# A projection moved from step 5 to step 3, and small products added in steps 4 and 12, in a one-core Perceiver layer

## What is computed

```python
Q, K, V = linear(query, Wq, bq), linear(ctx, Wk, bk), linear(ctx, Wv, bv)   # per head: 64 x 16, 1601 x 16
scores = Q @ K.T / sqrt(16)
feats = stack([scores.mean(), scores.max(-1).mean(), var(softmax(scores), ddof=1).mean()])  # per head
t = exp(clip(mlp(feats)))          # three small layers, two exact gelus: a temperature per head
attn = softmax(Q @ K.T / (2 * t))
out = linear(attn @ V, Wo, bo)
```

## Time and profile before

| | |
|---|---|
| median of three runs (lowest to highest) | 1311.03 us (1310.67 to 1316.09) |
| the profiled execution: its time | 1311.66 us |
| its span, first to last instruction | 1309.4 us |
| TensorE busy | 1155.3 us, 88% |
| VectorE, ScalarE, GpSimd busy | 822.0, 768.2, 403.0 us |
| mean granted TensorE clock | 0.861 |

### The profile page before, as it was taken

How to read it: one execution, slowest core, us unless ns; L and a number is a source line. 1 busy time by engine, 2 the same in 40 slices (tenths; PEclk the granted TensorE clock), 3 DMA queues, 4 the chain that set the end, 5 groups by cost and what they waited for, 6 DMA issues and landing times.

```text
span 1309.4 us, 39200 instructions
## 1 busy us (share of the span) xinstructions
PE 1155.3 (88%) x14964; PEld 928.9 (71%) x14964; DVE 822.0 (63%) x2124; ACT 768.2 (59%) x1547; POOL 403.0 (31%) x416
## 2 busy tenths in 40 slices
PE   3767898989899989999899989998999989998935
PEld 3545687868787877878687878787777878776622
DVE  3458665656666766767666766676776766772232
ACT  2434486757666765667566766676566756672300
POOL 2366441313234313333233323431333323301210
PEclk9868697969888987989798988899898979995865
DMA  4500110101010101010110101010101000000000
GB/s 122 187 19 25 29 26 14 54 22 35 14 38 10 50 11 42 19 34 26 26 35 14 46 7 45 11 50 10 42 19 35 26 17 3 3 11 2 2 5 4
DMA packets 46812, 38.85 MB, mean 30 GB/s; under 512 B 14576, under 2 KB 46000, under 8 KB 46640
## 3 DMA queue, kind: packets, MB, share of 16 engines
q1 hardware_dynamic: 46640, 36.41, 10.2%
HBM read 34.30 MB, written 2.10 MB: 28 GB/s over the span
## 4 chain that ended last, share of the span: by engine, by line
PE 65%; DVE 16%; issue 9%; ACT 5%; POOL 2%; DMA 1%; SPq 1%; DVEq 0%; ACTq 0%; POOLq 0%
PE pjp L605 11%; PE pjp L612 11%; PE s2p L677 10%; PE s1p L651 10%; PE pvp L694 7%; DVE est L1185 4%; DVE negm L1179 3%; PE tlp L808 2%; PE tlp L790 2%; PE tlp L784 2%; PE s2p L667 1%; PE tlp L751 1%; PE tlp L771 1%; DVE feat L1202 1%; ACT ering L909 1%
## 5 line engine op out<-in xcount | busy, mean ns | idle before, releaser
L1179 DVE TENSOR_REDUCE negm<-s1p 128x1 f32<-128x400 f32 (+1 forms) x512 | 289.3, 565 | 227.1 <-PE s1p L651 222.5
L909 ACT ACTIVATE ering<-s1p,negm 128x400 f32<-128x400 f32 (+1 forms) x512 | 305.6, 597 | 142.7 <-DVE negm L1179 138.0
L918 ACT ACTIVATE pring<-s2p 128x512 f32<-128x512 f32 (+1 forms) x448 | 251.9, 567 | 152.4 <-PE s2p L677 151.9
L651 PE MATMUL s1p<-kt,qbd 32*128 32x400 f32 (+1 forms) x1024 | 301.0, 597 | 15.8 <-ACT ering L909 13.7
L1185 DVE BATCH_NORM_STATS2 est<-ering 128x6 f32<-128x400 f32 (+1 forms) x512 | 290.3, 567 | 23.4 <-ACT ering L909 23.4
L605 PE MATMUL pjp<-cr,wkv 128*128 128x256 f32 (+1 forms) x1344 | 219.4, 321 | 70.6 <-ACT vt L869 45.7
L605 PEld LDWEIGHTS pjp<-cr,wkv 128*128 128x128 f32 x1344 | 196.1, 223 | 87.8 <-issue 58.5
L677 PE MATMUL s2p<-q2bd,kt 32*128 32x128 f32 (+1 forms) x3328 | 249.7, 284 | 0.0
L677 PEld LDWEIGHTS s2p<-q2bd,kt 32*128 32x128 f32 (+1 forms) x3328 | 240.6, 195 | 7.5
L1083 POOL TENSOR_TENSOR cr<-stage,cr 128x512 fp32r<-128x512 f32 (+1 forms) x112 | 132.0, 1179 | 268.7 <-ACT cr L900 268.7
L612 PE MATMUL pjp<-wkv,cr 128*128 128x256 f32 (+1 forms) x1200 | 191.8, 314 | 11.7 <-ACT kt L882 11.4
(11 more groups left out here) (186 smaller groups left out, 1008.8 us busy)
## 6 DMA issues: line engine op xcount, KB each, us to landing
stage<-in_ctx SPq DMA_DIRECT2D x96, 256.0 KB, 2.9
qbd<-q_dram SPq DMA_DIRECT2D x128, 8.0 KB, 1.7
stage<-in_ctx SPq DMA_DIRECT2D x16, 65.0 KB, 2.6
vt<-in_x SPq DMA_DIRECT2D x1, 1024.0 KB, 7.1
q_dram<-late SPq DMA_DIRECT2D x1, 1024.0 KB, 4.7
late<-in_x SPq DMA_DIRECT2D x8, 128.0 KB, 2.1
out_y<-late SPq DMA_DIRECT2D x8, 128.0 KB, 1.7
late<-in_gate SPq DMA_DIRECT2D x1, 768.0 KB, 5.0
```

Source lines behind the costliest of these rows:

```text
L651: nc.tensor.matmul(s1p[u % 3][:, 0:w], qbd[s.par][rows, g, :], kt[s.par][rows, g, lo:lo + w], start=True, stop=True).then_inc(s1_full, 1)
L909: nc.scalar.activation(ering[:, u % 3, 0:w], s1p[u % 3][:, 0:w], ACT.Exp, bias=negm[s.par][:, p, c:c + 1]).then_inc(s1_exp, 1)
L918: nc.scalar.activation(pring[0:m, v % NPR, 0:n], s2p[v % 2][0:m, 0:n], ACT.Exp).then_inc(s2_exp, 1)
L1179: nc.vector.tensor_reduce(negm[s.par][:, p, ch:ch + 1], s1p[u % 3][:, 0:w], AX.X, ALU.max, negate=True).then_inc(s1_max, 1)
```

## The change

The values' projection of context tile 4 is put in step 3 of a slot, where it was in step 5. Its place in the sequence of projections (between keys of tile 4 and keys of tile 5) stays. Then `fill` issues two products with 32 rows, 128 columns of weights and 256 streamed columns, in the row quarter that a second-pass unit of that step would use, behind the two score units of step 4 and of step 12, in slots 2 to 15. They write columns 256 to 511 of `pvp`, which nothing reads.

```diff
-PJ_PLAN = [(1, ("k", 4, 0)), (5, ("v", 4, 0)), (7, ("k", 5, 0)), (9, ("v", 5, 0)), (11, ("k", 6, 0)),
+PJ_PLAN = [(1, ("k", 4, 0)), (3, ("v", 4, 0)), (7, ("k", 5, 0)), (9, ("v", 5, 0)), (11, ("k", 6, 0)),
...
+FILL_AT = (S2_IDLE[0] - STEPS, S2_AT[-1] + 1 - STEPS)
...
+            def fill(s, u):
+
+
+                r = (S1_P[u] + 2) % PPB
+                rows = slice(RT * r, RT * r + RT)
+                for _ in range(2):
+                    nc.tensor.matmul(pvp[:, DB * P:2 * DB * P], qbd[s.par][rows, 0, :], kt[s.par][rows, 0, 0:DB * P],
+                                     start=False, stop=True, skip_group_check=True)
...
                             scores(s, step)
                             scores(s, step + 1)
+                            if step in FILL_AT and s.has(2, B - 1):
+                                fill(s, step)
```

## The result

The changed kernel takes 1266.6 us (median of four runs, 1254.6 to 1272.16) against 1311.09: a ratio of 0.964, 95% interval 0.957 to 0.971, 44.5 us faster. The forecast was 1256 us, 55 us faster, with a range of 1242 to 1270. The profiled execution took 1272.16 us, its span is 1269.9 us. A second profile of the same program, taken beside later experiments, took 1260.66 us: in that comparison the executions of the changed kernel lay within 19 us, those of the kernel before within 9, and the two profiles show what differs.

What follows compares the result with a forecast made beforehand. TensorE's work was taken to bound most of a slot, with a bank wait and low clock in steps 6 to 11; 1311.66 - 78 + 19 + 3.5 = 1256 us, range 1242 to 1270.

Steps and rivals of the forecast that it cites:

- What bounds the kernel: Most of a slot is TensorE's work; steps 6 to 11 have a 2.83 us wait and 10.4 us at 1.2 GHz.
- Part 1: Step 7's projection no longer waits for the emptied bank; step 8 starts 4.0 us earlier, at 559.1 in place of 563.08.
- Part 2: Step 8 to step 11 at full clock; 5.2 us a slot gained, 4.0 of them part 1: 78 us.
- Part 3: Low clock that returns in short thin stretches: one in three slots out of four, 1.7 us each, 19 us.
- Pieces A: The fifteen stretches from `temperature` 1 to the step-11 projection; the prediction had built one up to 8.4 us.
- slower: Rival: clock falls in step 5, which lost its 12 products, and stays down long; 1345 us, chance 0.06.
- Part 4: Added products stick out about 0.25 us behind step 12's score units; step 4's are covered: 3.5 us.
- pieces B: The fifteen stretches from the step-11 projection to the next `temperature` 1; only part 4's 3.5 us was added there.
- The clock falls as long as before: Rival: gap closed, but in thin steps 8 to 11 the clock falls for its 10 us; 1278 us, chance 0.15.
- All of the low stretch comes back: Rival: half the 10.4 us at half clock and the 2.83 us wait return, 8.0 a slot; 1192 us, chance 0.04.
- Nothing is gained: Rival: gain given back at a later wait for ScalarE or VectorE in the same slot; 1312 us, chance 0.06.
- The clock stays up: Rival: the fall comes from the gap alone, so nothing of part 3 is due; 1237 us, chance 0.17.

Runs made afterwards that it cites:

- the experiment with the filled wait: Kernel before the change, with four products of 128 rows and 256 columns ahead of the waiting projection in step 7: 1280.03 us, ratio 0.975.
- the version with wide products: Changed kernel plus unread products of 128 rows and 256 columns in steps 5 and 8, and in 11 and 15 of every second slot: 1243.58 us, ratio 0.945.

## Why the prediction came out as it did

**What bounds the kernel: right.** The wait for the emptied bank and the low clock behind it were the cost. Undoing the wait in either way gives the gain (0.965 and 0.962), keeping it and filling it gives 0.975, the added products alone nothing.

**Part 1, the wait: right.** Step 8 came 2.66 us after `temperature` 1, forecast 2.6, and what holds it there is ScalarE's exponential. The half microsecond of cover for the temperature chain was enough, in both kinds of slot: in the second, the first table load starts 7.24 us after the first score unit of step 2 (591.08 to 598.32), 7.22 us before the change (616.89 to 624.11).

**Part 2, 15 x 5.2 = 78 us: the mis-sized term, 8 us too high.** In the slot kind of the earlier trace rows the floor was 8.24 us, forecast 8.4; the difference is step 10, which takes 1.23 us at the full clock, not 1.4, since the clock was back at 569.2 and only 0.6 of its 1.53 us had been slow. But the term was one slot of one kind, times fifteen. Over the fifteen the piece took 197.3/15 = 13.15 us before, not 13.64, and six of the fifteen are of the kind with the products of the tail, whose floor is 8.88. All floors together are 9 x 8.24 + 6 x 8.88 = 127.4 us, and the term is 197.3 - 127.4 = 70 us in place of 78.

**Part 3, what comes back, 19 us: right in size, not in place.** Pieces A of the changed kernel lie 149.1 - 127.4 = 21.7 us above the floors in the first profile, 18.3 in the second. That the size fits is partly luck, since one of the places was not in the working. The prediction had looked for the thin place between steps 7 and 8. That one exists (the fall before step 9), but there is another: with its twelve products gone, step 5 waits up to 0.9 us for VectorE's statistics, and in every second slot the clock falls at step 6. I had named this place only in the slower rival, where the fall was to last 18 us; it lasts 6.8. I had read only one slot kind. There this wait is 0.22 us; in the other TensorE comes to `temperature` 0 earlier relative to VectorE's chain.

**Part 4, 3.5 us: if anything high.** 0.19 us stick out of step 12's pair, 14 x 0.19 = 2.7 us; over the whole stretch from step 11 to the next `temperature` 1 some 0.1 us of it is left.

**What the sum left out: pieces B.** They were to grow by part 4 alone and grew by 8.5 us in the first profile. In the loop a piece of the first kind takes 56.5 us in place of 55.6: the fall at step 6 begins in it, ahead of `temperature` 1. One of the second kind takes 61.0 on average in place of 59.4, with 6.8 us or more at 0.50 behind step 11 in every one. In the second profile these falls are fewer, B is 847.4, and pieces of the first kind are back at 55.6. So this term alone moves by 11 us between two executions of one program, and these profiles give no way to forecast it better than that.

In sum, against the first profile: 70 us of part 2 (forecast 78), 21.7 back (forecast 19), 8.5 for B (forecast 3.5), and 0.3 at the ends; that is 39.5 us of span against a forecast of 55.5. All the misses point the same way. The second profile gives 51.0 us, the medians 44.5: the forecast time is within the range of what executions differ by, the mechanism is as forecast, and the gain was set some 10 us too high.

**The rivals.** "The clock falls as long as before" is excluded: 3.4 and 6.8 us a slot in the loop, not 10.2. "All of the low stretch comes back" is excluded by the experiment with the filled wait: 3.5 us, not 5.2. "Nothing is gained" and "slower" are excluded by the time; in the second of these, step 8 at 561.4 has no row behind it (the projection of step 7, from 556.8 in 2.93 us, would end at 559.7), and its terms add up to 1346, not 1345. "The clock stays up" is what the version with wide products comes near, 1243.6 us at the price of its added work. The rule that puts such falls down to idle gaps (the Trainium skill, TensorE: Matmul & The Clock Gate, section Why this matters for your kernels) fits the longest, which went when the gap was closed or filled; at 539.9 the clock fell where no idle time over 0.4 us stands ahead.

## What to carry to other kernels

A bank with one buffer is held until its reader's engine has come through everything that stands ahead of the emptying, so look at what stands ahead of the emptying on the reader's engine (here two table loads), and move either side of it. When work is moved to close a gap, look at the place it has left: in a kernel whose TensorE clock falls in thin stretches, that place may be the next thin one. Read all kinds of slot, and not one: the slot read here was longer than the mean before, and its kind has the shorter floor. Products that nothing reads can be worth their time: here one wide product in step 5 gave 4 to 8 us, those of steps 5 and 8 together 20 to 24; the 32-row ones gave nothing alone and 8 to 9 us beside the wide ones.

## What the hardware showed that I had not expected

A stretch of 10.2 us at 1.2 GHz cost 3.0 to 3.5 us, a third of its length, since part of it was a wait in any case. The clock fell at places where TensorE had not been idle for more than 0.4 us but ran 32-row products and short products with V (ahead of 539.9 in the changed kernel). One program had executions from 1254.6 to 1274.4 us with the same order of work; in the two that were profiled the falls landed at different places.
